# Layer-0 attention: row sums copied to SBUF by ScalarE and inverted there in four pieces, the output scaled on GpSimd, the maximum units and projections in other slots

## The reference

```python
def _L0_attn_ref(x, w_q, w_k, w_v, w_u, b_u):      # x 4 x 1024 x 128, 16 heads of 64
    q = (x @ w_q).reshape(bs, n, h, hd); k = (x @ w_k).reshape(bs, n, h, hd); v = (x @ w_v).reshape(bs, n, h, hd)
    dot = jnp.einsum('bqhd,bkhd->bhqk', q * scale, k * scale)
    dot = jnp.where(causal, dot, -jnp.inf)
    att = jax.nn.softmax(dot, axis=-1)
    out = jnp.einsum('bhqk,bkhd->bqhd', att, v).reshape(bs, n, h * hd)
    return out @ w_u + b_u
```

## Time and profile before

| | us |
|---|---|
| median of 3 runs | 3159.69 (3151.41 to 3171.6) |
| the profiled execution | 3156.38 |
| its span in the trace | 3154.7 |
| layer-0 attention in it (first score at 59.67, last pair from 1438.72) | about the first 1495 |
| PE busy over the span | 2492.0 (79%) |
| DVE, ACT, POOL busy | 1566.6, 1220.0, 771.0 |

### The profile page before, as it was taken

How to read it: one execution, slowest core, us unless ns; L and a number is a source line. 1 busy time by engine, 2 the same in 40 slices (tenths; PEclk the granted TensorE clock), 3 DMA queues, 4 the chain that set the end, 5 groups by cost and what they waited for, 6 DMA issues and landing times. The chain is left out here.

```text
span 3154.7 us, 42629 instructions
## 1 busy us (share of the span) xinstructions
PE 2492.0 (79%) x15692; PEld 1480.2 (47%) x15692; DVE 1566.6 (50%) x3356; ACT 1220.0 (39%) x1692; POOL 771.0 (24%) x692
## 2 busy tenths in 40 slices
PE   5778887777877788787599998488888858874677
PEld 3434454444544445444388887233333334442454
DVE  3555546555465545564456667513222045445644
ACT  2323323333233332332133332266757735542331
POOL 1444434445344444454000000200000011000000
PEclk9989899899989888999589999599999979896889
DMA  1000000000000000000200000000000000002000
GB/s 58 1 1 1 1 1 1 1 1 1 1 1 1 1 1 1 1 1 1 51 0 0 0 0 0 3 1 1 1 0 0 1 3 1 1 1 62 0 1 27
DMA packets 35353, 17.87 MB, mean 6 GB/s; under 512 B 15226, under 2 KB 33028, under 8 KB 35204
## 3 DMA queue, kind: packets, MB, share of 16 engines
q1 hardware_dynamic: 35204, 15.86, 2.0%
HBM read 13.76 MB, written 2.10 MB: 5 GB/s over the span
## 5 line engine op out<-in xcount | busy, mean ns | idle before, releaser
L287 POOL TENSOR_TENSOR a_first<-a_first,a_ring 128x1024 f32<-128x1024 f32 (+3 forms) x320 | 549.3, 1717 | 251.7 <-ACT a_ring L492 154.4
L492 ACT ACTIVATE a_ring<-a_st 128x768 f32<-128x768 f32 (+1 forms) x256 | 235.0, 918 | 350.5 <-PE a_st L401 348.2
L1485 ACT ACTIVATE g_probsT<-g_s_ps 128x1024 f32<-128x1024 f32 (+2 forms) x320 | 282.7, 940 | 136.5 <-PE g_s_ps L1312 133.5
L416 PE MATMUL a_o_ps<-a_ring,a_v 128*64 128x512 f32 (+3 forms) x1280 | 277.4, 533 | 3.1 <-POOL a_ring L274 3.1
L540 DVE TENSOR_REDUCE a_part_max<-a_mx 128x2 f32<-128x1024 f32 x128 | 156.6, 1223 | 242.7 <-PE a_mx L372 242.3
L372 PE MATMUL a_mx<-a_k_hi,a_q_hi 64*128 64x512 f32 (+3 forms) x768 | 168.1, 462 | 123.1 <-DVE a_part_max L540 122.6
L563 DVE RECIPROCAL a_row_inv<-a_p_ps 128x512 f32<-128x512 f32 x64 | 214.8, 3357 | 58.2 <-PE a_p_ps L356 58.2
L916 PE MATMUL m_up<-m_xT_hi,m_w_hl 128*128 x640 | 211.7, 402 | 7.1 <-DVE m_glu L965 4.3
L949 ACT ACTIVATE m_silu<-m_up,m_bias 128x512 f32<-128x512 f32 x160 | 110.1, 688 | 238.8 <-PE m_up L916 238.8
L372 PEld LDWEIGHTS a_mx<-a_k_hi,a_q_hi 64*128 64x128 f32 x768 | 71.6, 197 | 273.5 <-DVE a_part_max L540 181.3
L274 POOL TENSOR_SCALAR_AFFINE_SELECT a_ring<-a_ring 128x256 f32<-128x256 f32 x224 | 88.9, 411 | 425.9 <-ACT a_ring L492 425.4
(11 more groups left out here) (338 smaller groups left out, 4364.3 us busy)
## 6 DMA issues: line engine op xcount, KB each, us to landing
m_w<-in_L_ffn_rw SPq DMA_DIRECT2D x2, 1024.0 KB, 8.5
s_w<-in_L_ffn_w SPq DMA_DIRECT2D x1, 2048.0 KB, 10.9
s_w<-in_L_ffn_w SPq DMA_DIRECT2D x4, 512.0 KB, 10.5
out_x<-x SPq DMA_DIRECT2D x4, 512.0 KB, 3.2
m_w<-in_L_ffn_rw SPq DMA_DIRECT2D x2, 512.0 KB, 7.6
x<-in_L_attn_x SPq DMA_DIRECT2D x1, 512.0 KB, 3.9
a_outT<-in_L_attn_w_q SPq DMA_DIRECT2D x1, 512.0 KB, 4.7
a_outT<-in_L_attn_w_k SPq DMA_DIRECT2D x1, 512.0 KB, 6.2
```

The source lines that it names most:

```text
L287: pool.tensor_tensor(total[:, :, q:q + w], total[:, :, q:q + w], probs_of(n, u)[:, :, off:off + w], ALU.add).then_inc(added, 1)
L416: last = pe.matmul(o_ps[rows_of(h), first_q:first_q + w], v_half[n // 4 % 2][:, j, head:head + A_HD], probs_of(n, u)[:, h, off:off + w], s ...
L492: act.activation(probs_of(n, u)[:, :, 0:w], st_ps[u % 2][:, :, 0:w], ACT.Exp).then_inc(exp_done, 1)
L1485: act.activation(out, src.rearrange("p k (j n) -> p k j n", j=at_once), ACT.Exp, scale=float(HD) ** -0.5).then_inc(exp_done, 1)
```

## The change

DVE no longer reads the row sums out of PSUM. ScalarE copies them to `row_inv[c]` (`keep_sums`), which is the point at which `p_ps` comes free; DVE inverts them there in four pieces of 128 columns, put at seven places of its loop by `INVERSES_BEFORE` (slot: chunk, first piece, last piece + 1); GpSimd multiplies `outT` by them (`scale_output`), ahead of its units 2 and 6 of the next pair. The tables of the maxima and projections change: the four projections stand in slots 0 to 3, and no maxima of a pair are left for its own slot 0. The sums of chunk 1 are computed in slot 1 in place of slot 2. `spread` shrinks to half, one chunk at a time. On ScalarE `keep_output` moves ahead of the other copies of its slot.

```diff
-MAXES_EARLY = {3: 0, 4: 1, 5: 2, 7: 3, 8: 4, 9: 6}
-MAXES_LATE = {8: 5, 9: 7}
-PROJECTIONS = {0: 0, 1: 1, 3: 2, 4: 3}
+MAXES_EARLY = {4: 2, 6: 3, 7: 5, 8: 7, 9: 9}
+MAXES_LATE = {2: 0, 3: 1, 6: 4, 7: 6, 8: 8}
+PROJECTIONS = 4
+INVERSES_BEFORE = {0: (0, 1, 3), 1: (0, 3, 4), 2: (1, 0, 1), 3: (1, 1, 2), 4: (1, 2, 3), 5: (1, 3, 4), 9: (0, 0, 1)}
...
-        row_inv = sb("row_inv", [P, HALF])
+        row_inv = [sb(f"row_inv{c}", [P, HALF]) for c in range(2)]
...
-        spread = sb("spread", [P, NB, P], F32R)
+        spread = sb("spread", [P, 4, P], F32R)
...
+                def scale_output(n, c):
+                    out = outT[:, n % OUT_SLOTS, c * HALF:(c + 1) * HALF]
+                    pool.wait_ge(o_kept, 2 * n + c + 1)
+                    pool.wait_ge(inv_ready, 4 * (2 * n + c + 1))
+                    pool.tensor_tensor(out, out, row_inv[c][:], ALU.mult).then_inc(out_kept, 1)
+
...
+                        if n and u == 2:
+                            scale_output(n - 1, 0)
+                        if n and u == 6:
+                            scale_output(n - 1, 1)
...
+                for c in range(2):
+                    scale_output(ALL_PAIRS - 1, c)
...
-                    take_shared(inv_ready, 2 * n + c + 1)
+                    take_shared(sums_kept, 2 * n + c + 1)
...
+                        if m < ALL_PAIRS and s in MAXES_EARLY:
+                            maxima(m, MAXES_EARLY[s])
                         if running and s > 0:
                             weigh(n, s - 1)
                         elif n > 0 and s == 0:
                             weigh(n - 1, UNITS_A_PAIR - 1)
                         if running and s == 0:
-                            maxima(n, 8)
-                        if running and s == 1:
                             turn_maxima(n, 1)
-                        if m < ALL_PAIRS and s in PROJECTIONS:
-                            project(m, PROJECTIONS[s])
-                        if n > 0 and s == 2:
+                        if m < ALL_PAIRS and s < PROJECTIONS:
+                            project(m, s)
+                        if n > 0 and s == 1:
                             add_rows(n - 1, 1)
                         if running and s == 5:
                             add_rows(n, 0)
+                        if m < ALL_PAIRS and s == 5:
+                            turn_maxima(m, 0)
                         for half, blk in values_of_slot(n, s):
                             project_values(half, blk)
                         for b, c in inputs_of_slot(n, s):
                             turn_input(b, c)
                         for b, t in outputs_of_slot(n, s):
                             output(b, t)
-                        if m < ALL_PAIRS and s in MAXES_EARLY:
-                            maxima(m, MAXES_EARLY[s])
-                        if m < ALL_PAIRS and s == 6:
-                            turn_maxima(m, 0)
-                        if running and s == 0:
-                            maxima(n, 9)
...
+                def keep_sums(n, c):
+                    act.wait_ge(summed, 2 * n + c + 1)
+                    if n:
+                        act.wait_ge(out_kept, 2 * (n - 1) + c + 1)
+                    act.activation(row_inv[c][:], p_ps[:], ACT.Copy).then_inc(sums_kept, 1)
...
+                        if n > 0 and s == 0:
+                            keep_output(n - 1, 1)
+                        if running and s == 3:
+                            keep_output(n, 0)
+                        if running and s == 0:
                             keep_shift(n, 1)
-                        if m < ALL_PAIRS and s in PROJECTIONS:
-                            keep_projection(m, PROJECTIONS[s])
+                        if m < ALL_PAIRS and s < PROJECTIONS:
+                            keep_projection(m, s)
+                        if n > 0 and s == 1:
+                            keep_sums(n - 1, 1)
+                        if running and s == 5:
+                            keep_sums(n, 0)
+                        if m < ALL_PAIRS and s == 5:
+                            keep_shift(m, 0)
...
-                    if m:
-                        dve.wait_ge(turned, 2 * (m - 1) + c + 1)
-                    out = spread[:, 4 * c:4 * c + 4, :].rearrange("p t (h n) -> p t h n", h=2)[:, :, :, 0]
+                    if 2 * m + c:
+                        dve.wait_ge(turned, 2 * m + c)
+                    out = spread[:].rearrange("p t (h n) -> p t h n", h=2)[:, :, :, 0]
                     dve.tensor_copy(out, largest[:, 4 * c:4 * c + 4, :]).then_inc(max_ready, 1)
 
-                def normalize_rows(n, c):
-                    dve.wait_ge(summed, 2 * n + c + 1)
-                    if 2 * n + c:
-                        dve.wait_ge(out_kept, 2 * n + c)
-                    dve.reciprocal(row_inv[:], p_ps[:]).then_inc(inv_ready, 1)
-                    dve.wait_ge(inv_ready, 2 * n + c + 1)
-                    dve.wait_ge(o_kept, 2 * n + c + 1)
-                    out = outT[:, n % OUT_SLOTS, c * HALF:(c + 1) * HALF]
-                    dve.tensor_tensor(out, out, row_inv[:], ALU.mult).then_inc(out_kept, 1)
+                def invert_sums(n, c, quarter):
+                    cols = slice(quarter * P, (quarter + 1) * P)
+                    dve.wait_ge(sums_kept, 2 * n + c + 1)
+                    dve.reciprocal(row_inv[c][:, cols], row_inv[c][:, cols]).then_inc(inv_ready, 1)
...
+                        if m < ALL_PAIRS and s in MAXES_EARLY:
+                            read_maxima(m, MAXES_EARLY[s])
+                        if m < ALL_PAIRS and s == 4:
+                            spread_maxima(m, 0)
+                        if m < ALL_PAIRS and s == 9:
+                            spread_maxima(m, 1)
+                        if m < ALL_PAIRS and s < PROJECTIONS:
+                            low_projection(m, s)
...
+                        if s in INVERSES_BEFORE:
+                            c, start, stop = INVERSES_BEFORE[s]
+                            of = n if s == 9 else n - 1
+                            for quarter in range(start, stop) if 0 <= of < ALL_PAIRS else ():
+                                invert_sums(of, c, quarter)
```

More of the change, by code:

```diff
@@ L140, in values_of_slot @@
     if n < 0:
[L141 removed]
+        groups = {4: (0, 1), 5: (2,), 6: (3, 4), 7: (5,), 8: (6,), 9: (7,)}
         return [(0, blk) for blk in groups.get(s, ())]
@@ L213, in attention_layer0 @@
         pv_done, o_kept = sem("pv_done"), sem("o_kept")
-        summed, inv_ready, out_kept = sem("summed"), sem("inv_ready"), sem("out_kept")
+        summed, sums_kept = sem("summed"), sem("sums_kept")
+        inv_ready, out_kept = sem("inv_ready"), sem("out_kept")
         y_done, y_kept = sem("y_done"), sem("y_kept")
@@ L378, in turn_maxima @@
                     for t in range(4):
-                        last = pe.matmul(mx_ps[:, 0, t * P:(t + 1) * P], spread[:, 4 * c + t, :], ident_r[:],
+                        last = pe.matmul(mx_ps[:, 0, t * P:(t + 1) * P], spread[:, t, :], ident_r[:],
                                          start=True, stop=True)
@@ L508, in _ @@
                             keep_input(b, c)
-                        if m < ALL_PAIRS and s == 6:
-                            keep_shift(m, 0)
-                        if n > 0 and s == 0:
-                            keep_output(n - 1, 1)
-                        if running and s == 3:
-                            keep_output(n, 0)
             @block.vector
@@ L610, in _ @@
                     for s in range(UNITS_A_PAIR):
-                        if running and s == 0:
-                            read_maxima(n, 8)
-                        if m < ALL_PAIRS and s in PROJECTIONS:
-                            low_projection(m, PROJECTIONS[s])
+                        if m < ALL_PAIRS and s in MAXES_EARLY:
[6 more added lines that the diff above has]
+                            low_projection(m, s)
                         for b, c in inputs_of_slot(n, s):
```

13 lines of the change are left out of this document (removed).

## The result

| | before | after |
|---|---|---|
| median | 3155.55 (3149.89 to 3171.6, 4 runs) | 2975.57 (2970.45 to 2977.38, 4 runs) |
| ratio | | 0.9419, 95% interval 0.9381 to 0.9457 |
| the profiled execution | 3156.38 | 2970.45 |
| first score of the stage | 59.67 | 61.37 |
| first score of the last pair | 1438.72 | 1248.24 |

The kernel is 5.8% faster, 180 us; 143 were forecast, and 3017 us stood where 2976 came, inside the range. Almost all of it lies between the first and the last pair: 1186.87 us in place of 1379.05, that is 192.2 less for 31 pairs. The lead before them is 1.7 longer, the last pair and its outputs 1.0, the rest of the program 3.5. Together that is the 186 between the two profiled executions.

What follows compares the result with a forecast made beforehand. PE was taken to bound layer-0 attention, with waits and time at the low clock to win. Waits -103, costs +7 and clock -47 sum to -143: 3013 on the profiled execution, 3017 us as median, range 2960 to 3090.

Steps and rivals of the forecast that it cites:

- waits, 31 pairs: PE's waits in layer-0 attention: 8.3 us a pair removed, 4.8 new, net 3.5; taken at 95% of 108, -103 us.
- clock: PE in layer-0 attention: less of the 276 us at 1.2 GHz, -47 us; granted clock 0.94 to 0.96.
- lead, last pair and the rest: Once each: extra maxima before the first scores +3.6, a product of 1.3 in the last pair, end costs; together +7 us.
- The walk from start to start: New order followed on PE with full-clock durations: 4.8 us of new waits, a clean pair of 35.6 us.
- six new waits: PE waits in the new order: 1.46 in slot 1, 1.1 in slot 4, 0.47, 0.72, 0.45 and 0.5 in slots 7 to 9.
- "I take half" of 94: Clock gain in the stage, set halfway between none and all, 0 and 94 us: -47 us.
- The price of low time: Loss in the 31 pairs per us at 1.2 GHz: 95 us for 276 us, 0.34 us each.
- the near end of the terms: Whole-kernel time if all of the clock is won: 2968 us; without any, 3064.
- Rival 1: DVE's spread CASTs wait for GpSimd's additions, up to 1.6 us each, some 2.3 a pair, 71 us: 3088; chance 0.14.
- a sign of being wrong: Clock at 0.90 or below, CASTs of 1 us and more the rule, or POOL behind with `weigh` waiting for cuts.
- Rival 2: DVE's in-place SBUF reciprocals collide with GpSimd; one piece in slot 0 held 1.6 us: 50 us, 3067; chance 0.07.
- Rival 3: Six smaller, more even waits a pair hold PE at 1.2 GHz; 1% slower, 3191, at clock 0.75; chance 0.06.

Runs made afterwards that it cites:

- The long wait put back: Changed kernel plus two spare reciprocals out of `p_ps` in slot 5, on which its next user waits: 3117.27 us, ratio 0.9845 against before.
- The release alone: Kernel before with ScalarE's copies, reciprocal pieces and GpSimd's product; maxima, projections and sums in their old slots: 3003.17 us, ratio 0.9503.
- the tables alone: Kernel before with only the maxima and their turn in the new slots; projections, sums, reciprocal and product as before: 3120.45 us, ratio 0.9852.
- the third unit a slot later: Changed kernel with the third maxima unit behind slot 4's weighing and chunk 0's spread moved to slot 5: 2959.69 us, ratio 0.9363 against before.
- the fastest kernel: Changed kernel with chunk 1's sums in slot 2 and the third maxima unit behind slot 4's weighing: 2920.11 us, ratio 0.9226 against before.

## Why the prediction was right, and where it was not

| term | forecast | shown |
|---|---|---|
| waits, 31 pairs | -103 | -90 |
| clock | -47 | -102 |
| lead, last pair and the rest | +7 | +6 |
| sum on the profiled execution | -143 | -186 |

**Waits: right in a pair, too many pairs.** The walk from start to start gave a clean pair of 35.6, and it is 35.83. All six new waits stand at their place and within 0.2 us. ScalarE frees `p_ps` as reckoned, and its 38 us of copies hold up nothing that shows. The sum took the saving in all 31 pairs, where the earlier trace rows has the wait of 2.95 only 28 times. The prediction saw the gap (7.6 us a pair in the stage against 7.97) and put it down to shorter waits at the low clock; three pairs without the 2.95 are most of it.

**Clock: mis-sized.** "I take half" of 94 is the step that failed. In the 31 pairs low time went from 263 us to 26, and the term came to 102 us, more than its far end. That the total is only 43 us off owes something to luck: the waits were over by 13 and the clock under by 55. The long wait put back shows why nearly all of the low time went: one wait of 3.2 us a pair holds the clock at 0.92 by itself. The release alone shows that this is not all: with the long waits gone but the maxima close behind each other at 1.32 each, the clock is 0.95. After has six waits in its clean pair, none above 1.41, and 0.99.

The Trainium skill ("TensorE: Matmul & The Clock Gate", section on oscillation) has the direction, that idle gaps beyond a certain length throttle. The direction agrees with these rows (2.95 and 3.2 us waits at 0.90 and 0.92, none above 1.41 at 0.99); but two waits of 1.32 close together stood ahead of the fall at 1202.5 in the release alone, so a short gap is not safe by its length alone, and the measurement decides.

**The price of low time: too small as well**, 0.34 against 0.42 in pairs of one kind. The prediction divided 95 us by 276. By windows of one microsecond there are 263, the clock of 0.90 being rounded. And the last three pairs, 4.5 us shorter than the clean one even at full clock, hide 13 us of the loss: (95 + 13) / 263 is 0.41. The long wait put back gives 0.37. The release alone has 49 us beyond its clean pairs for 93 us more of low time, 0.53 each, more than the low level can cost by itself (in a microsecond at 1.2 GHz half a microsecond of work is lost). Part of the 49 is therefore something else. PE waits 168.8 us in those 31 pairs in place of 155.6, though 4.1 and 4.2 in a clean one; the 13 us more lie mostly in the first pair and in those with layernorm or output work, and the 36 left are 0.39 each. One slip besides: the near end of the terms, all of the clock, is 2970 by their own sum where 2968 stands.

**The parts of the waits.** The forecast gave -4.48 us a pair to the release and +1.0 to the new order (3.8 removed at the four places of maxima, 4.8 of new waits). Shown are -3.96 for the release (35.12 against 39.08) and +0.71 for the order on top of it. In the clean pair the new order is a loss, as the walk had it. Its gain is elsewhere, mostly in the clock, 0.95 to 0.99 with the release in place, and in 13 us of shorter waits in the other pairs; that the prediction did not say. What the order costs or gives by itself stays open: the run with the tables alone moved only the maxima and has no clean pair.

**Rival 1, the spread waits for GpSimd: its mechanism came true, its price did not.** "CASTs of 1 us and more are the rule" was named as a sign of being wrong, and they are. The prediction's own walk had both CASTs inside an addition with 0.3 and 0.1 us to spare, so long CASTs were no sign against it. What is left is close to that: the CAST from 580.25 ends 0.36 us ahead of the turn at 582.67, and the one for chunk 1 in the same pair 0.36 ahead of its own. This is a narrow margin. With the third unit a slot later that slack is gone, and the same meeting costs up to 1.8 us in 8 places.

**Rival 2, the reciprocals in place collide with GpSimd: false.** 256 of them have a mean of 930 ns where 940 was reckoned, beside a POOL busy 60% of the stage, and the longest takes 953.

**Rival 3, the clock takes it back: false.** Smaller and more even waits do not add up to a low clock: 0.99.

**Left open.** What exactly separates a pair that falls to the low clock from one that doesn't. The same two waits of slot 1, 1.46 and 1.41 at 448.84 and 451.21 after, 1.44 and 1.41 in the kernel with the third unit late, left the clock at 1.00 in the one and 0.56 in the other. The four microseconds with the sums in them, first of after, then of that kernel:

```profile
450.14:454.14 4.00, 2.93 (x25) 1.45 (x25) 2.20 (x5) 1.63 (x3) 1.52 (x2) 1.00 0.02 4
```
```profile
446.13:450.13 4.00, 2.94 (x14) 1.32 (x16) 2.19 (x5) 0.88 (x2) 1.49 (x2) 0.56 0.01 4
```

So the waits of that place do not tell which way it goes. The spread of the fastest kernel's times, 2899.7 to 2935.6, is wider than that of after, 7 us. Its profiled execution is the slowest of the six: its 31 pairs are 50 us shorter than those of after, but what follows them took 1733.4 us in place of 1720.5, with 461 us of low time in place of 437. So in this execution some 13 us were lost behind the part that was changed; why wasn't tried.

## What to carry to other kernels

Where a busy TensorE runs at a clock of 0.90, count its time at the low level and price it apart, from pairs of the same kind with and without it (0.42 us for each here). One wait of 3.2 us a pair cost more than half again its own length through the clock, and a change of order that made the clean pair longer still made the kernel faster. A reciprocal out of a shared PSUM tile is worth a copy by an idle engine first. Of what moved with it, the engine of the product did not matter; the cut into pieces did, by some 16 us, since GpSimd's product waits for the last piece and its cuts wait behind the product. When a wait disappears, look whether it has only moved: with the tables alone 2.95 behind the reciprocal became 0.5 there and 2.5 behind the next read of the maxima. After such a change read PE's new waits: the largest of them, 1.41 us a pair, went by moving one call by one slot, and brought another 40 us.
